# One graph layer on one core: the edge sort's record in seven bf16 fields made by one operation, and reordered by a bf16 product

## The reference, cut to what matters

```python
xn = layernorm(x)                                             # 3125 x 256
msgs = edge_weight[:, None] * xn[dst]                         # one row per edge
agg = segment_sum(msgs, src, num_segments=3125)               # summed by the edge's first end
x = x + (agg @ gnn_W.T + gnn_b) + linear_attention_mix(xn)    # 8 heads, two layernorms, a 512 wide MLP
x = x + top2_of_16_experts(layernorm(x))                      # SiLU-gated experts, 512 wide
```

## Time and profile before

| | |
|---|---|
| median of 3 runs | 1322.45 us (1321.16 to 1322.45) |
| the profiled execution, its own time | 1325.14 us |
| its span | 1323.4 us |
| PE busy | 1148.7 us (87% of the span) |
| DVE busy | 850.8 us (64%) |
| ACT busy | 537.1 us (41%) |
| POOL busy | 621.3 us (47%) |
| mean granted PE clock | 0.939 |

### The profile page before, as it was taken

The page is one execution under the profiler, slowest core; times in us unless marked ns, Lnnn a source line. Parts: engine busy times, 40 slices in busy tenths (PEclk is TensorE's granted clock), DMA queues, the critical chain, the costliest instruction groups (busy, mean ns, idle before and its releaser), DMA issues.

```text
span 1323.4 us, 21724 instructions
## 1 busy us (share of the span) xinstructions
PE 1148.7 (87%) x6831; PEld 1016.0 (77%) x6831; DVE 850.8 (64%) x1960; ACT 537.1 (41%) x1247; POOL 621.3 (47%) x624
## 2 busy tenths in 40 slices
PE   6998798999989899898998998741999999999980
PEld 5897686787868778687786886641999999999970
DVE  8644788888888888988889877857222222222226
ACT  4747575573856648466483742211011111111100
POOL 5845447566575755657566471004233333333320
PEclk9899899999999999999999999755999999999995
DMA  7213123222222222222222231205699999999948
GB/s 208 82 55 109 54 63 93 68 82 71 72 80 68 89 66 83 72 68 84 68 85 72 64 97 32 79 19 178 232 331 332 327 340 333 335 327 336 329 158 284
DMA packets 118372, 196.12 MB, mean 148 GB/s; under 512 B 13526, under 2 KB 67604, under 8 KB 118292
## 3 DMA queue, kind: packets, MB, share of 16 engines
q1 hardware_dynamic: 88958, 120.62, 27.5%
q0 software_dynamic: 26112, 71.34, 17.1%
q10 hardware_dynamic: 3222, 3.20, 0.7%
HBM read 177.12 MB, written 17.99 MB: 147 GB/s over the span
## 4 chain that ended last, share of the span: by engine, by line
PE 54%; DVE 21%; DVEq 10%; issue 8%; ACT 3%; DMA 2%; SPq 1%; ACTq 0%; POOL 0%; POOLq 0%
PE psum L978 17%; PE psum L988 8%; PE psum L902 6%; DVE agg L1212 5%; DVE agg L1218 4%; PE psum L912 3%; PE psum L721 3%; PE psum L695 3%; PE psum L789 2%; PE psum L739 2%; ACT in_slot L382 2%; PE psum L841 2%; DVE hot L1205 2%; DVEq L1297 1%; DVEq L1085 1%
## 5 line engine op out<-in xcount | busy, mean ns | idle before, releaser
L633 POOL DMA_INDIRECT arena<-y_rows,gather_i x416 | 440.6, 1059 | 301.6 <-PE psum L902 121.1
L902 PE MATMUL psum<-arena,hot 128*128 128x256 f32 x832 | 222.6, 397 | 15.9 <-DVE hot L1205 6.7
L1212 DVE TENSOR_TENSOR agg<-psum,agg 128x256 f32 x416 | 174.5, 420 | 44.8 <-DVE agg L1212 20.9
L479 ACT ACTIVATE arena<-arena,listed 128x256 f32<-128x256 f32 x416 | 175.6, 498 | 65.6 <-DMA arena<-y_rows,gather_i 65.5
L902 PEld LDWEIGHTS psum<-arena,hot 128*128 128x128 f32 x832 | 151.4, 195 | 53.1 <-issue 23.8
L978 PEld LDWEIGHTS psum<-arena 128*128 128x128 f32 x1536 | 181.4, 194 | 4.9 <-issue 2.5
L978 PE MATMUL psum<-arena 128*128 128x128 f32 x1536 | 181.9, 277 | 2.0 <-DVE arena L1531 2.0
L1538 DVE TENSOR_TENSOR arena<-psum,arena 128x512 f32<-128x512 f32 x64 | 44.3, 692 | 204.9 <-PE psum L978 204.9
L569 ACT ACTIVATE arena<-psum 128x512 f32<-128x512 f32 x64 | 38.3, 598 | 335.1 <-PE psum L978 335.1
L655 POOL DMA_INDIRECT chosen_rows<-arena,back_at x64 | 63.4, 990 | 219.7 <-DVE arena L1545 215.0
L382 ACT ACTIVATE in_slot<-iota,place_f 128x128 f32<-128x128 f32 x416 | 127.3, 390 | 62.2 <-DVE place_f L1073 62.0
(11 more groups left out here) (208 smaller groups left out, 1662.4 us busy)
## 6 DMA issues: line engine op xcount, KB each, us to landing
arena<-in_L_ffn_w_dram SPq DMA_DIRECT2D x144, 512.0 KB, 5.6
xnT<-in_L_ffn_w_dram SPq DMA_DIRECT2D x48, 512.0 KB
arena<-y_rows,gather_i POOLq DMA_INDIRECT x416, 2.8
arena<-chosen_rows SPq DMA_DIRECT2D x8, 640.0 KB, 8.9
y_rows<-w ACTq DMA_DIRECT2D x6, 512.0 KB, 2.9
agg<-in_x_dram SPq DMA_DIRECT2D x4, 640.0 KB, 6.7
n_rows<-arena SPq DMA_DIRECT2D x4, 640.0 KB
out_dram<-agg SPq DMA_DIRECT2D x4, 640.0 KB
```

What stands on the lines that cost most here:

```text
L479: last = act.activation(rows[h][:, t, :], rows[h][:, t, :], ACT.Copy, scale=weight[h][:, t:t + 1])
L633: pool.indirect_dma_start(rows[h][:, t, :], None, y_rows, bass.IndirectOffsetOnAxis(ap=gather_i[h][:, t:t + 1], axis=0)).then_inc(gathered ...
L902: pe.matmul(bank_of(g, t // 2)[:, (t % 2) * C:(t % 2 + 1) * C], hot[:, n % HOTS, :], rows[h][:, t, :], start=True, stop=True).then_inc(met, 1)
L1212: dve.tensor_tensor(own, bank_of(g, t // 2)[:, (t % 2) * C:(t % 2 + 1) * C], own, ALU.add).then_inc(evicted, 1)
```

## The change

Each end of an edge is kept as two bf16 pieces (the upper six bits in place, and the lower six bits), and the weight as three bf16 pieces (rounded, the rest rounded, the rest of that). Seven fields in bf16 take the place of three in fp32. The pieces are laid out in pairs of edge columns (`pieces[P, 208, 7, 2]`), and so are `in_tile` (`[P, 4, 32, 2]`) and `record` (`[P, 4, 7, 32, 2]`), so that the innermost run of every operand is at least two neighbouring elements. `make_field` (12 operations of 256 elements a group) becomes `make_record` (4 operations of 1792 elements a group, at steps 24, 30, 39 and 48). `in_bin`, `in_tile`, `in_slot` and `record` are bf16, and the product of line 695 is bf16 with 224 columns, read with a step of two elements. `read_list` and `place_list` add the pieces in fp32. The start converts the edges with more operations, and POOL makes two more constants ahead of `consts_ready`.

```diff
-    FIELDS = 3
+    FIELDS = 7
+    LOW = 64
...
-        in_bin = sb("in_bin", [P, BINS, GE])
+        weight_in = sb("weight_in", [P, COLS])
+        edge_part = sb("edge_part", [P, 2, COLS], I32)
+        pieces = sb("pieces", [P, COLS // 2, FIELDS, 2], BF16)
+        piece = [pieces[:, :, f, :] for f in range(FIELDS)]
+        bin_b = sb("bin_b", [P, COLS], BF16)
+        bin_no = sb("bin_no", [P, BINS, GE], BF16)
+        tile_of = sb("tile_of", [P, GT, 2], BF16)
+        in_bin = sb("in_bin", [P, BINS, GE], BF16)
-        in_tile = sb("in_tile", [P, CH, GT])
-        record = [sb(f"record{k}", [P, CH, FIELDS, GT]) for k in range(2)]
-        in_slot = [sb(f"in_slot{k}", [P, CH, P]) for k in range(2)]
+        in_tile = sb("in_tile", [P, CH // 2, GT, 2], BF16)
+        record = [sb(f"record{k}", [P, CH // 2, FIELDS, GT, 2], BF16) for k in range(2)]
+        in_slot = [sb(f"in_slot{k}", [P, CH, P], BF16) for k in range(2)]
+        place_b = sb("place_b", [P, GE], BF16)
...
+            pool.iota(bin_no[:, :, :], [[1, BINS], [0, GE]], base=0, channel_multiplier=0, ...)
+            pool.iota(tile_of[:, :, :], [[1, GT], [0, 2]], base=0, channel_multiplier=0, ...)
...
-                    last = pe.matmul(in_order, in_slot[k % 2][:, c, :], record[k % 2][:, c, :, :].rearrange("p f t -> p (f t)"),
+                    last = pe.matmul(in_order, in_slot[k % 2][:, c, :], record[k % 2][:, c // 2, :, :, c % 2].rearrange("p f t -> p (f t)"),
...
             def mark_bins(g):
-                dve.tensor_tensor(in_bin[:, :, :], edges_of(bin_f, g).unsqueeze(1).to_broadcast([P, BINS, GE]),
-                                  iota[:, 0:BINS].unsqueeze(2).to_broadcast([P, BINS, GE]), ALU.is_equal)
+                dve.tensor_tensor(in_bin[:, :, :], edges_of(bin_b, g).unsqueeze(1).to_broadcast([P, BINS, GE]),
+                                  bin_no[:, :, :], ALU.is_equal)
...
+                dve.tensor_copy(place_b[:, :], place_i[:, 1, :])
                 dve.tensor_scalar(place_f[:, :], place_i[:, 2, :], -1.0, None, ALU.mult).then_inc(places_ready, 1)
...
+            def make_record(g, k):
+                dve.drain()
+                if g * CHUNKS + k >= 2:
+                    dve.wait_ge(reordered, g * CHUNKS + k - 1)
+                first = (g * GE + k * CH) // 2
+                own = pieces[:, first:first + CH // 2, :, :].rearrange("p a f b -> p (a f) b")
+                tiles = in_tile[:, :, :, :].rearrange("p a t b -> p a (t b)")
+                dve.tensor_tensor(record[k % 2][:, :, :, :, :].rearrange("p a f t b -> p a f (t b)"),
+                                  tiles.unsqueeze(2).to_broadcast([P, CH // 2, FIELDS, 2 * GT]),
+                                  own.unsqueeze(2).to_broadcast([P, CH // 2 * FIELDS, GT, 2]), ALU.mult).then_inc(record_ready, 1)
...
             def read_list(g):
-                dve.tensor_copy(gather_i[h][:, :], in_order[:, GT:2 * GT])
-                dve.tensor_copy(listed[h][:, :, :], in_order.rearrange("p (f t) -> p f t", f=FIELDS)[:, 0:3:2, :])
+                part = in_order.rearrange("p (f t) -> p f t", f=FIELDS)
+                dve.tensor_copy(parts[:, :, :], part[:, 1:FIELDS:2, :])
+                dve.drain()
+                dve.tensor_tensor(node[h], part[:, 0, :], parts[:, 0, :], ALU.add)
+                dve.tensor_tensor(gather_i[h][:, :], part[:, 2, :], parts[:, 1, :], ALU.add)
+                dve.tensor_tensor(weight[h], part[:, 4, :], parts[:, 2, :], ALU.add)
...
             def place_list(g):
+                dve.tensor_tensor(weight[h], in_order[:, 6 * GT:7 * GT], weight[h], ALU.add)
...
-            dve.tensor_copy(edge[:, 0, :], edge_i[:, 0, :])
-            dve.tensor_copy(edge[:, 1, :], edge_i[:, 1, :])
-            dve.drain()
+            dve.tensor_copy(piece[4], weight_in[:, :]...)
+            for end in range(2):
+                dve.tensor_scalar(edge_part[:, 0, :], edge_i[:, 1 - end, :], LOW * (LOW - 1), None, ALU.bitwise_and)
+                dve.tensor_scalar(edge_part[:, 1, :], edge_i[:, 1 - end, :], LOW - 1, None, ALU.bitwise_and)
+                dve.drain()
+                dve.tensor_copy(piece[2 - 2 * end], edge_part[:, 0, :]...)
+                dve.tensor_copy(piece[3 - 2 * end], edge_part[:, 1, :]...)
+                dve.drain()
             dve.tensor_scalar(edge_i[:, 0, :], edge_i[:, 0, :], 7, None, ALU.arith_shift_right)
-            dve.drain()
-            dve.tensor_copy(bin_f, edge_i[:, 0, :])
+            for k in range(2):
+                dve.tensor_tensor(weight_in..., weight_in..., piece[4 + k], ALU.subtract)
+                dve.drain()
+                dve.tensor_copy(piece[5 + k], weight_in[:, :]...)
+                dve.drain()
+            dve.tensor_copy(bin_b[:, :], edge_i[:, 0, :])
...
-                for k, at_steps in enumerate(((23, 24, 27), (29, 30, 32), (36, 39, 43), (46, 48, 49))):
-                    if step in at_steps:
-                        make_field(g, k, at_steps.index(step))
+                if step in (24, 30, 39, 48):
+                    make_record(g, (24, 30, 39, 48).index(step))
```

More of the change, by code:

```diff
@@ L140, in gps_layer @@
         cross_row = [sb(f"cross_row{h}", [1, CROSS], I32) for h in range(2)]
+        parts = sb("parts", [P, 3, GT])
         gather_i = [sb(f"gather_i{h}", [P, GT], I32) for h in range(2)]
@@ L281, in _ @@
             sp.wait_ge(edges_padded, 1)
-            for a, b in ((edge_i[:, 0, :], src), (edge_i[:, 1, :], dst), (edge[:, 2, :], edge_weight)):
+            for a, b in ((edge_i[:, 0, :], src), (edge_i[:, 1, :], dst), (weight_in[:, :], edge_weight)):
                 for first, end in ((0, EVEN), (EVEN, P - 1)):
@@ L574, in _ @@
             pool.memset(edge_i[96:P, :, LAST_ROW:COLS], 0)
-            pool.memset(edge[96:P, 2, LAST_ROW:COLS], 0.0)
+            pool.memset(weight_in[96:P, LAST_ROW:COLS], 0.0)
             pool.drain().then_inc(edges_padded, 1)
@@ L1085, in mark_tiles @@
                 dve.drain()
-                dve.tensor_tensor(in_tile[:, :, :], place_i[:, 1, own].unsqueeze(2).to_broadcast([P, CH, GT]),
-                                  iota[:, 0:GT].unsqueeze(1).to_broadcast([P, CH, GT]), ALU.is_equal)
-            def make_field(g, k, f):
-                if f == 0:
-                    dve.drain()
-                    if g * CHUNKS + k >= 2:
-                        dve.wait_ge(reordered, g * CHUNKS + k - 1)
-                last = dve.tensor_tensor(record[k % 2][:, :, f, :], in_tile[:, :, :],
-                                         edges_of(edge[:, f, :], g, k).unsqueeze(2).to_broadcast([P, CH, GT]), ALU.mult)
-                if f == FIELDS - 1:
-                    last.then_inc(record_ready, 1)
+                whole = [P, CH // 2, GT, 2]
+                two = place_b[:, own].rearrange("p (a b) -> p a b", b=2)
+                dve.tensor_tensor(in_tile[:, :, :, :], two.unsqueeze(2).to_broadcast(whole), tile_of[:, :, :].unsqueeze(1).to_broadcast(whole),
+                                  ALU.is_equal)
+            def make_record(g, k):
[8 more added lines that the diff above has]
+                                  own.unsqueeze(2).to_broadcast([P, CH // 2 * FIELDS, GT, 2]), ALU.mult).then_inc(record_ready, 1)
             def make_records(g, k):
                 mark_tiles(g, k)
-                for f in range(FIELDS):
-                    make_field(g, k, f)
+                make_record(g, k)
             def read_list(g):
@@ L1162, in _ @@
             dve.wait_ge(edges_loaded, 144)
-            dve.tensor_copy(edge[:, 0, :], edge_i[:, 0, :])
-            dve.tensor_copy(edge[:, 1, :], edge_i[:, 1, :])
-            dve.drain()
-            dve.tensor_scalar(edge_i[:, 0, :], edge_i[:, 0, :], 7, None, ALU.arith_shift_right)
-            dve.drain()
-            dve.tensor_copy(bin_f, edge_i[:, 0, :])
+            dve.tensor_copy(piece[4], weight_in[:, :].rearrange("p (a b) -> p a b", b=2))
+            for end in range(2):
+                dve.tensor_scalar(edge_part[:, 0, :], edge_i[:, 1 - end, :], LOW * (LOW - 1), None, ALU.bitwise_and)
+                dve.tensor_scalar(edge_part[:, 1, :], edge_i[:, 1 - end, :], LOW - 1, None, ALU.bitwise_and)
+                dve.drain()
+                dve.tensor_copy(piece[2 - 2 * end], edge_part[:, 0, :].rearrange("p (a b) -> p a b", b=2))
+                dve.tensor_copy(piece[3 - 2 * end], edge_part[:, 1, :].rearrange("p (a b) -> p a b", b=2))
+                dve.drain()
+            dve.tensor_scalar(edge_i[:, 0, :], edge_i[:, 0, :], 7, None, ALU.arith_shift_right)
+            for k in range(2):
+                dve.tensor_tensor(weight_in[:, :].rearrange("p (a b) -> p a b", b=2), weight_in[:, :].rearrange("p (a b) -> p a b", b=2), piece[4 + k], ALU.subtract)
+                dve.drain()
+                dve.tensor_copy(piece[5 + k], weight_in[:, :].rearrange("p (a b) -> p a b", b=2))
+                dve.drain()
+            dve.tensor_copy(bin_b[:, :], edge_i[:, 0, :])
             dve.drain()
```

9 lines of the change are left out of this document (5 added, 4 removed).

## The result

Slower: 1326.56 us (median of 6 runs, 1326.27 to 1329.34) against 1321.81 us of the kernel before in the same comparison (1318.52 to 1322.8); ratio 1.0039, 95% interval [1.0026, 1.0052]. The forecast had said 1318.5 us and "faster". The time lies in its range, the sign is wrong. The profiled execution took 1329.34 us, with a span of 1327.6 us and a mean clock of 0.929.

The account below looks back on a forecast made before the run. It saw a ring of DVE, ACT and PE, with PE owning the smaller part. Loop 11 x (-0.6 + 0.25) = -3.9 us and start 0 gave 1321.2 us profiled, 2.69 lower as median: 1318.5 us, range 1302 to 1345.

Parts of the forecast that it names:

- The product's size: In PE's chunks of records, the bf16 product was to cut a chunk from 1.76 to 0.77 us.
- The record: On DVE, the new 1792-element bf16 operation was priced by bytes at 1.09 us.
- The by-elements rival: The record on DVE goes by elements, 2.01 us each, giving 1344 us in all; chance 0.14.
- `mark_bins`: On DVE, this 800-element operation was to fall by bytes from 0.98 to 0.57 us.
- DVE's stretch behind step 39: The part of the period where DVE ends last, up to `place_f`: +0.2 to +0.3 us a period.
- the -0.6 us a period for PE's stretch: From `query` some 12 us on, where PE ends last: one cheaper chunk was to save 0.6 us a period.
- the records of steps 24 and 30 lie where DVE waits for PE anyway: In PE's stretch, these two longer DVE operations were claimed to be covered and cost nothing.
- the 1.64 us that DVE waited at step 39: DVE's wait at 343.83 us, at the end of PE's stretch, was read as a wait for PE's product.
- ACT's 0.63 us at `std`: ACT's idle time ahead of `std(1, g)` was taken as the slack that ends the gain at 0.6 us.
- The clock: Rival: PE, 3 us a period more idle, has its clock fall in each period, +9 us, 1328; chance 0.12.
- `place_b` ahead of `place_f`: At the end of DVE's stretch, this added copy was priced at +0.1 us, all on the path.
- The start: Ahead of the loop, PE's 6.3 us stall less 2.5 absorbed and 3.8 from chunks: 0 (-4 to +5).

Follow-up runs that it names:

- before_half: The kernel before with only 4 of the 8 products of each chunk, half of the edges left out: 1304.15 us, 0.9886.
- after_thin: The changed kernel with 4 of 8 products a chunk and loop records of 896 elements instead of 1792: 1333.64 us, 0.9979, in a comparison with remote waits.
- after_bins: The changed kernel with DVE's reading of 32 bin numbers into registers moved from step 38 to step 42: 1324.2 us, 0.9976.
- after_pad: The changed kernel with four idle products put into each chunk of the loop's sorts: 1335.78 us, 1.011.
- after_top: The changed kernel with the register reading at step 42, `place_f` ahead of the `place_b` copy, and six idle 256-column products before `query`: 1304.56 us, 0.9862.
- after_first: The changed kernel with the `place_b` copy moved behind `place_f`: 1360.98 us, 1.0185, in a comparison with remote waits.
- after_again: The changed kernel, unedited, measured once more: 1326.31 us, 1.0031.
- before_top: The kernel before with the register reading at step 42 and six idle 256-column products before `query`: 1334.76 us, 0.9989, in a comparison with remote waits.
- after_top2: The kernel of after_top again, beside before_top: 1330.24 us, 0.9948, in a comparison with remote waits.

## Why the prediction was wrong

- *The product's size: right.* Forecast 0.77 us a chunk between starts; the 8 records start over 0.80 us. In periods without a fall PE's busy time is 3.3 us lower (50.9 and 47.7 in the mean), for a forecast of 4.0.
- *The record: right.* 1.09 us forecast, 1.092 measured. That is the estimate by the Trainium skill's packed way too ("VectorE: DVE Perf Modes", section "Mode 2x_1P"), so the trace agrees with it. The "Vector Engine (DVE) Microarchitecture Reference" of the Trainium skill, section 5.1, has one element read again and again at one a cycle, and a row read again and again packed; the operation, with rows of two, fits the second. The by-elements rival is out.
- *`mark_bins`: right.* 0.57 forecast, 0.565 measured. DVE's stretch behind step 39: +0.25 forecast, +0.30 measured.
- *The failed step is the -0.6 us a period for PE's stretch, in its "the records of steps 24 and 30 lie where DVE waits for PE anyway", which priced DVE's work there at nothing.* The forecast took the 1.64 us that DVE waited at step 39 for slack all through, and let ACT's 0.63 us at `std` end the gain. Most of the 1.64 was the register reading; the slack that it left was 0.57 us (before_half). For the product alone, that would nearly have given the 0.6, by another limit than the one named. But DVE's additions used it up. The reading begins 11.8 to 11.9 us after `place_f` where PE holds nothing up (before_half, periods without a fall), and 12.31 in the changed kernel: the longer records. It begins at 12.52 in the periods where `place_f` takes 0.38 us. What were single fields of 0.42 us between evictions are operations of 1.09 us there, and halving them brought 0.47 back (after_thin). At step 39 that leaves 0.0 in the one kind of period and -0.2 in the other, instead of -0.6. after_bins, which moves the reading and nothing else, gave 0.89 us back at that very place.
- *The clock: a rival, under-rated.* It had 0.12 for a fall in each period, +9 us. The falls went from four periods in ten to seven, +4.7 to +6.8 us. Why they come oftener stays open. A less busy PE does not explain it: with 485.2, 488.6, 512.9 and 515.3 us of PE work in ten periods, there are four falls (before_half), seven (after), seven (after_pad) and four (before).
- *`place_b` ahead of `place_f`: under-priced.* Forecast 0.1 us. `place_f` went from 0.18 to 0.38 us behind the copy in seven of ten periods, and in those `query` begins 4.53 us after it, for 4.34 before (4.32 in the other three). The periods with it are 0.57 us longer than those without (55.94 and 55.37), of which this explains 0.2; the rest is open.
- *The start: too cautious.* The stall was 5.75 us (forecast 6.3), the cadence of the first four chunks fell from 6.13 to 5.1 us, with ACT's 5.1 as its floor, and the fourth began at 74.24 us for 74.43. So far that is the forecast. The later four, counted at nothing, gave 3.6 us more (the last begins at 113.97 for 117.75): -4.4 us in all for a forecast of 0.
- *The sum.* Forecast loop -3.9, measured +8.5: 12.4 us off. A period without a fall was forecast at -0.35 and came out at +0.14 to +0.35, 5.4 to 7.7 us in eleven: that is the lost 0.6 (6.6 us), give or take the small terms. The falls are 4.7 to 6.8. The start's 4.4 us hid a third of it, which is luck: without it the time would be some 1331 us. Either miss alone would have left the kernel at 1320 to 1322 us, no slower than before; it took both to make it slower.

## What to carry to other kernels

A wait on a semaphore can hide work of the waiting engine's own sequencer. Before a gain of the engine waited for is counted, look in the chain (here DVEq) for register readings that lie inside that wait: what is left of it is at most the slack. And where a small operation becomes a long one, each place it is moved to is to be priced against that remainder. Where a clock falls in some periods and not in others, a change has to be measured with the falls taken away and with them, and its runs read beside their granted clocks.

## What the runs showed of the hardware

- Six idle fp32 products of 256 columns before `query` took away every fall of the granted clock in the ten periods, in all seven runs that had them (`query` at most 1.99 us); eleven of 24 columns, which filled nearly the same wait, took away none (3.64 us at 330.56).
- A two-tensor operation with all operands in bf16, one of them read in rows of two elements that repeat, ran 1792 elements in 1.09 us and 896 in 0.63 us: 0.52 ns an element, half of the 1.03 ns of fp32.
- Loading 32 registers from SBUF on DVE's sequencer took 2.10 us each time in the loop, and 2.35 us ahead of it. No busy time holds it, and DVE's next instruction began 0.12 us behind its end where nothing else held it.
- The small conversion of `place_f` took 0.38 us in seven of ten periods where another small one came just before it on DVE, 0.17 us in the other three, and 0.18 us wherever it came first; in after_top it is the copy, now second, that takes 0.38 us in most. What tells the periods apart is open.
- In some comparisons waits "released by remote" appear, in kernels of one core, as in after_first:
```profile
508.69 0.99 DVE L1065 SCALAR_TENSOR_TENSOR count<-psum,count 128x800 f32<-128x800 f32 x1 [2.19 <-remote]
```
  They do not belong to a chip: one chip showed none in after_again, after_bins and after_top, and later 8 in before_top and 24 in after_top2. The kernel before takes 1336 to 1338 us there instead of 1322. What releases them is open.
